# A state-space and expert layer on one core: the last norm's inverse square root joined with two others in the next chunk's group 4, its output added in group 9

## The chip, the cores and the metric

The kernel runs on one core of a Trainium2 chip. The time is device microseconds (us) of one execution. Engines are named as in the profile: PE is the matrix engine (PEld its weight loads), DVE the vector engine, ACT the scalar engine, POOL the GpSimd engine, SP the engine that issues most transfers. All five run their own instruction queue in order and meet at semaphores only.

## What is computed

The input is 8 sequences of 1024 tokens with 256 features in float32. Cut to its core, the reference is

```
x = x + layernorm(mamba(layernorm(x)))      # conv, selective scan, gate, out projection
x = x + layernorm(experts(layernorm(x)))    # 16 experts, 4 of them chosen for each token
layernorm(v) = (v - mean(v)) / sqrt(var(v) + 1e-5)
```

The change touches the outermost norm of the second line, the one behind the experts, and where the sum with x is made.

## The kernel before

The tokens are cut into NC = 16 chunks of 512 tokens, two for each sequence. A chunk lies as 4 blocks (b) of 128 tokens by 256 features, so a statistic of a chunk is a tile of 128x4.

The work is one software pipeline, written out by hand. Every engine runs the same loop over periods p = -2 to 17, and in each over 16 groups g = 0 to 15; G = 16p + g counts the groups. A period carries several chunks at different stages: the scan and its read-out are of chunk p, the input norm (names `e_`) of chunk p + 2, the front part with convolution, dt and gate (names `f_`) of chunk p + 1, the norm and the routing behind the mamba part (names `p_`) of chunk p - 1, the experts run 26 groups behind the scan, and the last norm (names `z_`) was of chunk p - 2. The order inside a group is the order of the `if` lines in each engine's loop; nothing is scheduled automatically. Periods with an odd p are the second half of a sequence and start each scan from the tile carry, periods with an even p save into carry on ACT (L607).

What one group does in the steady state:

- DVE: `expert_gate` (th<-th,Gp, L1007), one scan of 128x512 (L897), `expert_up` (th<-Up,th, L1012), three more scans, then the group's small extras, then `inputs` (L883): hs<-dxr,Bb, 128x2048, which writes the products that the next group scans.
- ACT: four decays dA<-dtr,A (L511) into the two PSUM banks dA0 and dA1, tanh for one expert (L517), and extras. A decay waits until the scan that reads its bank is done.
- POOL: waits until `inputs` of its group is done, then issues the transfer if there is one, weighs one expert (th<-th,cmb, L762) and multiplies the scanned states by C (`read_out`, hs<-hs,Cb, 128x2048, L782). The states read are those of the group before.
- PE: read-out sums, the gate and up products of one expert, the down product of an earlier one, and one projection.

The inverse square root is a bit trick and three Newton steps: `newton` (L813 to L822) is 11 dependent tiny DVE instructions. `variance` (L826) and `shift` (L829) make the input of it and the bias behind it. In group 4, DVE already joins two of them: the two roots of the input norm of chunk p + 2 and the root of chunk p - 1 lie side by side in ep_w, 12 columns, and one `newton` serves all. The `q` root in group 6 stands alone (`p_scale2`).

The last norm of chunk p - 2 before the change, all inside period p: `z_my` in group 11 copies the expert sums from PSUM to my (L674), `z_squares` in group 12 makes the squares (L529, XB<-my,z_s), `z_scale` in group 12 on DVE makes variance, `newton` and shift on z_w with 4 columns, `z_norm` in group 12 on ACT scales my (L685, four instructions), directly ahead of `f_silu_z` (L587, which loads another activation table ahead of it and one behind it), and `add_out` in group 13 on POOL issues the transfer that adds my to the output in DRAM (L772, 512 KB). `z_my` of the next chunk waits until this transfer has landed, since it writes my again.

In group 9, DVE runs `route_groups` and `route_experts` (L944 to L1003) behind the four scans: 31 small instructions on tiles of 128x64 and less in SBUF, which choose the experts; behind them come `y_out` (L904) and `inputs` (L883) of group 10. In ACT's group 8 stand two copies `p_x2T` (L655) with decays and tanh between them.

Of the kernel before, what the change touches and what calls it, by code (L numbers as in the profile page):

```python
# [14 lines left out]
TB = CH // P  # L15
# [60 lines left out]
def sandwich_kernel(nc, x, w_in, w_out, w_gu, w_dn, w_x, w_rt, cols, alog, ebias, consts, sel_dt, out):  # L76
    with ExitStack() as ctx:
# [70 lines left out]
        p_s = sb('p_s', [P, 3, TB])  # L148
        b_s = sb('b_s', [P, 3, TB])
        p_w = sb('p_w', [P, 3, TB])  # L150
        ep_w = sb('ep_w', [P, 3, 3 * TB])
        p_nb = sb('p_nb', [P, TB])
        top8 = sb('top8', [P, TB, 8])
        comb = sb('comb', [P, TB * NE])
# [20 lines left out]
        p_act = Steps(sem('p_act'), ['xn0', 'xn1', 'rev0', 'rev1', 'nm', 'sq', 'ro', 'sum2', 'nm2', 'sq2', 'x2', 'x2T0', 'x2T1', 'sig', 'cmT'])  # L175
        m_g, m_u, m_d, m_th, m_v, m_w, m_a = (sem(k) for k in ('m_g', 'm_u', 'm_d', 'm_th', 'm_v', 'm_w', 'm_a'))
        z_act = Steps(sem('z_act'), ['my', 'nm', 'sq', 'zn'])
        z_dve = Steps(sem('z_dve'), ['w1'] + rsqrt_names('r') + ['nb'])
        ld_w, ld_w2, w_act, w_dve = (sem(k) for k in ('ld_w', 'ld_w2', 'w_act', 'w_dve'))
        ld_xin = sem('ld_xin')  # L180
        ld_x = [sem(f'ld_x{k}') for k in range(2)]
# [316 lines left out]
        def _(act):  # L498
# [45 lines left out]
            def e_norm(c):  # L544
                act.wait_ge(e_dve.sem, e_dve.at(c, 'nbr'))
                for b in range(TB):
                    ins = act.activation(xin[:, b, :], xin[:, b, :], ACT.Identity, scale=ep_w[:, 1, 2 * TB + b:2 * TB + b + 1], bias=e_nb[:, b:b + 1])
                ins.then_inc(e_act.sem, 1)

            def e_xT(p, q):  # L550
# [85 lines left out]
            def p_ro(p):  # L636
                c = p - 1
                act.wait_ge(p_dve.sem, p_dve.at(c, 'nb'))
                for b in range(TB):
                    ins = act.activation(rn[:, b, :], rn[:, b, :], ACT.Identity, scale=ep_w[:, 1, b:b + 1], bias=p_nb[:, b:b + 1])  # L640
                ins.then_inc(p_act.sem, 1)

            def p_x2(p):
# [38 lines left out]
            def z_norm(c):  # L682
                act.wait_ge(z_dve.sem, z_dve.at(c, 'nb'))
                for b in range(TB):
                    ins = act.activation(my[:, b, :], my[:, b, :], ACT.Identity, scale=z_w[:, 1, b:b + 1], bias=z_nb[:, b:b + 1])  # L685
                ins.then_inc(z_act.sem, 1)
            for p, g, G in groups():
                F, R_ = (in_f(p), in_p(p))
                q = expert_at(G)
                if 0 <= p < NC:  # L690
                    decay(G * NBETA + 2)
                    decay(G * NBETA + 3)
                if R_ and g in (3, 4):
# [24 lines left out]
                if R_ and g in (0, 1):  # L718
                    p_xn(p, g)
                if 0 <= p + 2 < NC and g == 2:  # L720
                    e_sums(p + 2)
                if 0 <= p + 2 < NC and g == 3:
                    e_squares(p + 2)
                if R_ and g == 5:
                    p_sums2(p)
                    p_squares2(p)
                if R_ and g == 4:
                    p_ro(p)
                if F and g in (6, 11):
                    f_z(p, {6: 0, 11: 3}[g])  # L730
                if F and g == 6:
                    f_silu(p)
                if R_ and g == 6:
                    p_x2(p)
                if F and g == 7:
                    f_xd(p)
                if in_e(p) and g == 7:
                    e_norm(p + 2)
                if R_ and g == 8:
                    p_x2T(p, 1)  # L740
                if F and g == 9:
                    f_softplus(p)
                if R_ and g == 10:
                    p_cmT(p)
                if g == 11 and 0 <= p - 2 < NC:
                    z_my(p - 2)
                if g == 12 and 0 <= p - 2 < NC:
                    z_norm(p - 2)
                if F and g == 12:
                    f_silu_z(p)  # L750
                if in_e(p) and g == 13:
                    e_xT(p, 0)
                if in_e(p) and g in (14, 15):
                    f_b(p, g - 14)

        @block.gpsimd
        def _(pool):
# [25 lines left out]
            for p, g, G in groups():  # L783
                if 0 <= G < NGRP:
                    pool.wait_ge(s_u, G + 1)
                if in_p(p) and g == 5:
                    add_x1(p - 1)
                if g == 13 and 0 <= p - 2 < NC:
                    add_out(p - 2)
                q = expert_at(G - 2)  # L790
                if q is not None:
# [5 lines left out]
        def _(dve):  # L797
# [33 lines left out]
            def e_var(c):  # L831
                dve.wait_ge(e_act.sem, e_act.at(c, 'sq'))
                if c > 0:
                    dve.wait_ge(e_act.sem, e_act.at(c - 1, 'xr'))
                dve.tensor_scalar(ep_w[:, 0, TB:2 * TB], e_s[:, 1, :], 1.0 / DM, LN_EPS, ALU.mult, ALU.add).then_inc(e_dve.sem, 1)
                dve.tensor_scalar(ep_w[:, 0, 2 * TB:3 * TB], e_s[:, 1, :], (1.0 + RMS_EPS) / DM, LN_EPS * RMS_EPS, ALU.mult, ALU.add).then_inc(e_dve.sem, 1)

            def e_scale(c):
                rs, rr = (ep_w[:, 1, k * TB:(k + 1) * TB] for k in (1, 2))
                dve.tensor_scalar(ln1[:, c, 0, :], rs, 1.0, None, ALU.mult).then_inc(e_dve.sem, 1)  # L840
                dve.tensor_tensor(ln1[:, c, 1, :], e_s[:, 2, :], rs, ALU.mult).then_inc(e_dve.sem, 1)
                dve.tensor_tensor(e_nb[:, :], e_s[:, 2, :], rr, ALU.mult).then_inc(e_dve.sem, 1)
# [178 lines left out]
            for p, g, G in groups():
# [14 lines left out]
                if F and g in (2, 3):  # L1036
                    conv(p, g - 2)
                if g == 4 and (R_ or 0 <= p + 2 < NC):
                    c0, c1 = (0 if R_ else TB, 3 * TB if 0 <= p + 2 < NC else TB)
                    if 0 <= p + 2 < NC:  # L1040
                        e_var(p + 2)
                    if R_:
# [6 lines left out]
                        p_scale(p)  # L1049
                    if 0 <= p + 2 < NC:  # L1050
                        e_scale(p + 2)
                if R_ and g == 6:
                    p_scale2(p)
                if R_ and g == 9:
# [46 lines left out]
```

## Time and profile before

| | us |
|---|---|
| median of 3 runs | 2755.98 |
| lowest and highest of them | 2751.46, 2756.31 |
| the profiled execution, its own time | 2754.25 |
| its span | 2752.5 |
| DVE busy | 2434.5 (88%) |
| PE busy | 2418.8 (88%) |
| ACT busy | 1633.1 (59%) |
| POOL busy | 1511.1 (55%) |

Busy times are of the profiled execution. A period of the steady state takes about 158 us, a group 8 to 13. The rows of a timeline read: start in us from the span's start, duration in us, engine, line, operation, output<-inputs, shapes, count; in brackets the idle time of the engine ahead of it and the engine and line that ended it. Rows of one kind that touch are merged, their start is the first one's.

### The profile page before, as it was taken

Reading aid. Unit: us, or ns where it says so; the run is one execution under the profiler, and the core shown is the slowest. Engines: PE = TensorE matmul, PEld = TensorE weight load, DVE = VectorE, ACT = ScalarE, POOL = GpSimd, SP = SyncE. Lnnn points to the kernel's source line nnn. Section 1 sums busy time; section 2 is a strip of 40 time slices with the busy share of each in tenths; the row PEclk is TensorE's granted clock in tenths of the full one; section 3 lists DMA queues with packets and bytes.
Section 4 is the critical chain, followed back from the end, with each engine's and each line's share of the span. In section 5 each row is a group of like instructions: output and inputs, shape, how many; then the busy total and the mean of one; then the engine's idle time right before and its main releaser. Section 6 shows DMA issues by size and latency. Waiting matters only on the chain.

```text
span 2752.5 us, 27115 instructions
## 1 busy us (share of the span) xinstructions
PE 2418.8 (88%) x8416; PEld 1183.5 (43%) x8416; DVE 2434.5 (88%) x3233; ACT 1633.1 (59%) x3312; POOL 1511.1 (55%) x548
## 2 busy tenths in 40 slices
PE   4556799998989999998999999898999989888987
PEld 1112254453545444444544445453544545443554
DVE  1699999999999999999999999999999999999532
ACT  3565656666665667566566667666566666644321
POOL 0255565655556565655656565565656555565422
PEclk9777899999999999999999999999999999999999
DMA  1623253534344343524435353443535343442232
GB/s 35 231 86 124 94 177 93 180 118 153 114 134 155 118 158 118 183 87 156 140 115 177 101 176 109 144 137 103 186 93 179 118 155 105 137 157 80 68 87 56
DMA packets 175563, 353.43 MB, mean 128 GB/s; under 512 B 16283, under 2 KB 82108, under 8 KB 166972
## 3 DMA queue, kind: packets, MB, share of 16 engines
q1 hardware_dynamic: 164668, 334.93, 36.3%
q0 software_dynamic: 10752, 16.78, 3.7%
q8 instruction: 67, 1.10, 0.2%
q14 instruction: 76, 0.62, 0.1%
HBM read 291.35 MB, written 51.90 MB: 125 GB/s over the span
## 4 chain that ended last, share of the span: by engine, by line
DVE 57%; issue 19%; ACT 15%; PE 7%; POOL 1%; DMA 1%; DVEq 0%; SPq 0%; POOLq 0%; ACTq 0%
DVE hs L897 26%; DVE hs L883 12%; DVE th L1007 5%; DVE th L1012 4%; ACT DX L529 2%; DVE XC L856 2%; PE Gp L424 2%; ACT dA L511 1%; ACT L511 1%; PE Up L432 1%; PE FP L351 1%; PE FP L361 1%; ACT XC L582 1%; ACT SZ L587 1%; ACT XB L529 1%
## 5 line engine op out<-in xcount | busy, mean ns | idle before, releaser
L782 POOL TENSOR_TENSOR hs<-hs,Cb 128x2048 f32<-128x2048 f32 x256 | 1170.6, 4572 | 199.8 <-DVE hs L883 199.8
L511 ACT ACTIVATE dA<-dtr,A 128x512 f32<-128x512 f32 x1024 | 701.8, 690 | 827.9 <-DVE hs L897 826.9
L762 POOL TENSOR_TENSOR th<-th,cmb 128x512 f32<-128x512 f32 x256 | 338.1, 1325 | 803.4 <-DVE hs L883 711.8
L897 DVE TENSOR_TENSOR_SCAN hs<-dA,carry,hs 128x512 f32<-128x512 f32 x512 | 627.7, 1265 | 19.8 <-ACT dA L511 19.4
L424 PE MATMUL Gp<-x2T,Wgu 128*128 128x512 f32 x1024 | 532.6, 645 | 115.2 <-DVE th L1007 115.1
L897 DVE TENSOR_TENSOR_SCAN hs<-dA,hs 128x512 f32<-128x512 f32 x512 | 596.1, 1203 | 31.6 <-ACT dA L511 31.1
L883 DVE TENSOR_TENSOR hs<-dxr,Bb 128x2048 f32<-128x2048 f32 x256 | 601.9, 2351 | 12.5 <-DMA dxr<-dx_d 12.5
L432 PE MATMUL Up<-x2T,Wgu 128*128 128x512 f32 x1024 | 492.7, 604 | 0.0
L442 PE MATMUL MY<-Wdn,th 128*128 128x256 f32 x2048 | 486.4, 380 | 0.2 <-POOL th L762 0.2
L442 PEld LDWEIGHTS MY<-Wdn,th 128*128 128x128 f32 x2048 | 383.5, 190 | 137.4 <-issue 94.7
L424 PEld LDWEIGHTS Gp<-x2T,Wgu 128*128 128x128 f32 x1024 | 182.2, 196 | 449.5 <-issue 253.6
L351 PE MATMUL FP<-xT,Win 128*128 128x512 f32 x512 | 270.2, 653 | 74.1 <-ACT XB L601 40.3
L432 PEld LDWEIGHTS Up<-x2T,Wgu 128*128 128x128 f32 x1024 | 196.4, 196 | 265.0 <-issue 227.6
L454 PE MATMUL Y<-hs,Cst 128*32 128x512 f32 x2048 | 283.2, 626 | 27.4 <-POOL hs L782 27.4
L1007 DVE SCALAR_TENSOR_TENSOR th<-th,Gp 128x512 f32<-128x512 f32 x256 | 173.6, 678 | 73.6 <-ACT th L517 73.6
L517 ACT ACTIVATE th<-Gp 128x512 f32<-128x512 f32 x256 | 148.3, 579 | 88.7 <-PE Gp L424 88.7
L351 PEld LDWEIGHTS FP<-xT,Win 128*128 128x128 f32 x512 | 98.0, 203 | 222.2 <-issue 99.5
L1012 DVE TENSOR_TENSOR th<-Up,th 128x512 f32<-128x512 f32 x256 | 170.2, 665 | 10.5 <-PE Up L432 10.0
L387 PE MATMUL FP<-Wout,SZ 128*128 128x256 f32 x512 | 123.9, 386 | 6.1 <-ACT DX L622 6.1
L361 PE MATMUL FP<-XB,Kdiag 128*128 128x512 f32 x256 | 120.4, 614 | 6.1 <-ACT XB L560 6.1
L387 PEld LDWEIGHTS FP<-Wout,SZ 128*128 128x128 f32 x512 | 99.0, 194 | 35.0 <-issue 15.7
L454 PEld LDWEIGHTS Y<-hs,Cst 128*32 128x32 f32 x2048 | 40.8, 109 | 155.2 <-issue 113.3
(131 smaller groups left out, 1820.5 us busy)
## 6 DMA issues: line engine op xcount, KB each, us to landing
dtr<-dt_d SPq DMA_DIRECT2D x64, 1024.0 KB, 5.7
dxr<-dx_d SPq DMA_DIRECT2D x128, 512.0 KB, 7.5
cmb<-cm_d SPq DMA_DIRECT2D x256, 256.0 KB, 3.7
Wdn<-in_w_dn SPq DMA_DIRECT2D x256, 128.0 KB, 3.6
dt_d<-XB SPq DMA_DIRECT2D x16, 1024.0 KB, 4.3
dx_d<-DX SPq DMA_DIRECT2D x16, 1024.0 KB, 5.9
Bb<-bc_d SPq DMA_DIRECT2D x64, 256.0 KB, 3.0
Cb<-bc_d SPq DMA_DIRECT2D x64, 256.0 KB, 4.0
```

What stands on the lines that cost most here:

```text
L351: mm = pe.matmul(FP[:, :], Win[:, q, c0:c0 + P], xT[:, q, :], start=q == 0, stop=q == KM - 1)
L424: mm = pe.matmul(Gp[:, :], Wgu[:, k, e, 0:DE], x2T[:, c % 2, k, :], start=k == 0, stop=k == KM - 1)
L432: mm = pe.matmul(Up[:, :], Wgu[:, k, e, DE:2 * DE], x2T[:, c % 2, k, :], start=k == 0, stop=k == KM - 1)
L442: mm = pe.matmul(MY[b // 2][:, (b % 2) * DM:(b % 2 + 1) * DM], th[:, q % NTH, b * P:(b + 1) * P], Wdn[:, q % NWD, :], start=e == 0 and b % ...
L454: mm = pe.matmul(Y[beta * CB:(beta + 1) * CB, :], sel_y, hs[:, G % NH, beta, :], start=False, stop=s == NSIG - 1, tile_position=(0, beta * ...
L511: act.activation(dA[h % 2][:, :], dtr[:, M % 2, beta, :], ACT.Exp, scale=A[:, k:k + 1]).then_inc(s_dA, 1)
L762: pool.tensor_tensor(th[:, q % NTH, :], th[:, q % NTH, :], cmb[:, q % 2, :], ALU.mult).then_inc(m_a, 1)
L782: pool.tensor_tensor(hs[:, G % NH, :, :], hs[:, G % NH, :, :], Cb[:, s, :].unsqueeze(1).broadcast_to([P, NBETA, CH]), ALU.mult).then_inc(s ...
L883: dve.tensor_tensor(hs[:, G % NH, :, :], dxr[:, M % 2, :, :], Bb[:, s, :].unsqueeze(1).broadcast_to([P, NBETA, CH]), ALU.mult).then_inc(s_ ...
L897: dve.tensor_tensor_scan(hv, dA[h % 2][:, :], hv, first, ALU.mult, ALU.add).then_inc(s_h, 1)
L1007: dve.scalar_tensor_tensor(out=th[:, q % NTH, :], in0=th[:, q % NTH, :], scalar=1.0, in1=Gp[:, :], op0=ALU.add, op1=ALU.mult).then_inc(m_v, 1)
L1012: dve.tensor_tensor(th[:, q % NTH, :], Up[:, :], th[:, q % NTH, :], ALU.mult).then_inc(m_w, 1)
```

## The change

The tile ep_w gets 16 columns instead of 12. The two roots of chunk p + 2 move to columns 0 to 7, the root of chunk p - 1 to columns 8 to 11, and columns 12 to 15 take the root of the last norm of chunk p - 3. For chunks 0 to 13, `z_scale` in group 12 is gone from DVE: variance is made in group 4 of the next period, the joined `newton` serves it too, and the shift is made behind the others. `z_norm` moves from group 12 to group 8 of the next period on ACT, and `add_out` from group 13 to group 9 of the next period on POOL, ahead of the weighing and the read-out of that group. The last two chunks stay as they were.

```diff
-        ep_w = sb('ep_w', [P, 3, 3 * TB])
+        ep_w = sb('ep_w', [P, 3, 4 * TB])
...
             def z_norm(c):
                 act.wait_ge(z_dve.sem, z_dve.at(c, 'nb'))
                 for b in range(TB):
-                    ins = act.activation(my[:, b, :], my[:, b, :], ACT.Identity, scale=z_w[:, 1, b:b + 1], bias=z_nb[:, b:b + 1])
+                    rs = z_w[:, 1, b:b + 1] if c >= NC - 2 else ep_w[:, 1, 3 * TB + b:3 * TB + b + 1]
+                    ins = act.activation(my[:, b, :], my[:, b, :], ACT.Identity, scale=rs, bias=z_nb[:, b:b + 1])
...
-                if g == 12 and 0 <= p - 2 < NC:
+                if g == 8 and 0 <= p - 3 < NC - 2:
+                    z_norm(p - 3)
+                if g == 12 and NC - 2 <= p - 2 < NC:
                     z_norm(p - 2)
...
-                if g == 13 and 0 <= p - 2 < NC:
+                if g == 9 and 0 <= p - 3 < NC - 2:
+                    add_out(p - 3)
+                if g == 13 and NC - 2 <= p - 2 < NC:
                     add_out(p - 2)
...
                 if g == 4 and (R_ or 0 <= p + 2 < NC):
-                    c0, c1 = (0 if R_ else TB, 3 * TB if 0 <= p + 2 < NC else TB)
+                    Z = 0 <= p - 3 < NC - 2
+                    c0, c1 = (0 if 0 <= p + 2 < NC else 2 * TB, (4 if Z else 3 if R_ else 2) * TB)
+                    if Z:
+                        z_var(p - 3, ep_w[:, :, 3 * TB:])
+                        dve.wait_ge(z_dve.sem, z_dve.at(p - 3, 'w1'))
...
+                    if Z:
+                        shift(z_dve, z_nb, z_s, ep_w[:, :, 3 * TB:])
...
-                if g == 12 and 0 <= p - 2 < NC:
+                if g == 12 and NC - 2 <= p - 2 < NC:
                     z_scale(p - 2)
```

The order of the instructions at the places that matter follows; line numbers of the changed kernel are 1 to 6 higher than before.

POOL in period 3, groups 8 to 12 and the start of 13, before. L762 is the weighing, L782 the read-out, L772 the transfer of the last norm:

```order
L762 TENSOR_TENSOR th<-th,cmb 128x512
L782 TENSOR_TENSOR hs<-hs,Cb 128x2048
L762 TENSOR_TENSOR th<-th,cmb 128x512
L782 TENSOR_TENSOR hs<-hs,Cb 128x2048
L762 TENSOR_TENSOR th<-th,cmb 128x512
L782 TENSOR_TENSOR hs<-hs,Cb 128x2048
L762 TENSOR_TENSOR th<-th,cmb 128x512
L782 TENSOR_TENSOR hs<-hs,Cb 128x2048
L762 TENSOR_TENSOR th<-th,cmb 128x512
L782 TENSOR_TENSOR hs<-hs,Cb 128x2048
L772 DMA out<-my 128x4x256
L762 TENSOR_TENSOR th<-th,cmb 128x512
```

and the same queue now, groups 8 to 10 of period 3 (L766, L786 and L776 are the same three):

```order
L766 TENSOR_TENSOR th<-th,cmb 128x512
L786 TENSOR_TENSOR hs<-hs,Cb 128x2048
L776 DMA out<-my 128x4x256
L766 TENSOR_TENSOR th<-th,cmb 128x512
L786 TENSOR_TENSOR hs<-hs,Cb 128x2048
L766 TENSOR_TENSOR th<-th,cmb 128x512
L786 TENSOR_TENSOR hs<-hs,Cb 128x2048
```

The transfer stood ahead of the weighing of group 13; it now stands ahead of that of group 9, one period later.

ACT now, from the first x2T copy of group 8 to the sigmoid's exponential of group 9, in period 3 (before, the same rows without L687):

```order
L656 ACTIVATE x2T<-FP 128x512
L512 ACTIVATE dA<-dtr,A 128x512 x2
L518 ACTIVATE th<-Gp 128x512
L656 ACTIVATE x2T<-FP 128x512
L687 ACTIVATE my<-my,z_nb,ep_w 128x256 x4
L512 ACTIVATE dA<-dtr,A 128x512 x2
L661 ACTIVATE DX<-FP 128x64
```

The four instructions of `z_norm` stand behind the last extra of group 8, ahead of group 9's decays. In group 12 they are gone from between tanh (or the save into carry) and the table load of `f_silu_z`.

DVE now, group 4 of period 3, from the last scan to the start of the joined root:

```order
L903 SCALAR_TENSOR_TENSOR hs<-dA,carry,hs 128x512 [waits s_dA] x3
L832 TENSOR_SCALAR ep_w<-z_s 128x4 [waits z_act]
L841 TENSOR_SCALAR ep_w<-e_s 128x4 [waits e_act,z_dve]
L842 TENSOR_SCALAR ep_w<-e_s 128x4
L832 TENSOR_SCALAR ep_w<-p_s 128x4 [waits p_act]
L819 TENSOR_SCALAR ep_w<-ep_w 128x16 [waits e_dve,p_dve]
```

The first L832 is new, ahead of the other three inputs; the joined root has 16 columns instead of 12, and one L835 (z_nb<-z_s,ep_w) is new behind the other results, directly ahead of `inputs`.

## Rows read from the trace of the kernel before

**Rows 1.** The page: the chain of waits that ended last, shares by engine.

```profile
DVE 57%; issue 19%; ACT 15%; PE 7%; POOL 1%; DMA 1%; DVEq 0%; SPq 0%; POOLq 0%; ACTq 0%
```

**Rows 2.** Groups by line, then waits (total us, times, longest): z_norm.

```profile
L685 ACT ACTIVATE my<-my,z_nb,z_w 128x256 f32<-128x256 f32 x64 | 33.2, 589 | 16.8 <-DVE z_nb L829 16.8
...
ACT my L685 <- DVE z_nb L829: 16.8, 16, 2.6
```

**Rows 3.** Timeline, groups 12 and 13 of an even period.

```profile
1439.59 4.53 POOL L782 TENSOR_TENSOR hs<-hs,Cb 128x2048 f32<-128x2048 f32 x1
...
1444.72 0.17 DVE L826 TENSOR_SCALAR z_w<-z_s 128x4 f32<-128x4 f32 x1 [0.77 <-ACT XB L529]
...
1446.29 0.20 ACT L607 ACTIVATE carry<-hs 128x4 f32<-128x4 f32 x1
...
1447.18 2.28 DVE L883 TENSOR_TENSOR hs<-dxr,Bb 128x2048 f32<-128x2048 f32 x1
1447.30 2.07 ACT L685 ACTIVATE my<-my,z_nb,z_w 128x256 f32<-128x256 f32 x4 [0.81 <-DVE z_nb L829]
...
1449.39 1.28 ACT L587 ACT_TABLE_LOAD   x1
...
1450.02 1.33 POOL L772 DMA_DIRECT2D out<-my  x1 [5.90 <-DVE hs L883]
...
1452.09 5.03 POOL L782 TENSOR_TENSOR hs<-hs,Cb 128x2048 f32<-128x2048 f32 x1
...
1454.63 2.34 DVE L897 TENSOR_TENSOR_SCAN hs<-dA,hs 128x512 f32<-128x512 f32 x2 [1.73 <-ACT dA L511]
```

**Rows 4.** Timeline, groups 8 and 9 of an odd period.

```profile
1562.11 0.59 ACT L655 ACTIVATE x2T<-FP 128x512 f32<-128x512 f32 x1
...
1564.46 4.53 POOL L782 TENSOR_TENSOR hs<-hs,Cb 128x2048 f32<-128x2048 f32 x1
...
1564.98 0.69 ACT L511 ACTIVATE dA<-dtr,A 128x512 f32<-128x512 f32 x1 [2.28 <-DVE hs L897]
...
1568.98 0.17 DVE L944 TENSOR_SCALAR DX<-DX 128x64 f32<-128x64 f32 x1
...
1569.77 0.22 DVE L948 TENSOR_TENSOR DX<-DX,Ebias 128x64 f32<-128x64 f32 x1
```

**Rows 5.** Timeline, groups 8 and 9 of an even period.

```profile
1403.71 0.58 ACT L655 ACTIVATE x2T<-FP 128x512 f32<-128x512 f32 x1
...
1406.10 4.53 POOL L782 TENSOR_TENSOR hs<-hs,Cb 128x2048 f32<-128x2048 f32 x1
...
1410.40 0.29 DVE L944 TENSOR_SCALAR DX<-DX 128x64 f32<-128x64 f32 x1
```

**Rows 6.** Timeline, group 5 of an even period: a late read-out and inputs.

```profile
421.20 4.80 POOL L782 TENSOR_TENSOR hs<-hs,Cb 128x2048 f32<-128x2048 f32 x1
...
423.76 4.40 DVE L883 TENSOR_TENSOR hs<-dxr,Bb 128x2048 f32<-128x2048 f32 x1
```

**Rows 7.** Timeline, inputs in group 13 of period 15.

```profile
2555.42 3.40 DVE L883 TENSOR_TENSOR hs<-dxr,Bb 128x2048 f32<-128x2048 f32 x1
```

**Rows 8.** Groups by line: a step of the joined root; waits: DVE in group 4.

```profile
L820 DVE TENSOR_TENSOR ep_w<-ep_w 128x12 f32<-128x12 f32 (+2 forms) x57 | 9.6, 169 | 1.9
...
DVE ep_w L826 <- ACT DX L529: 28.8, 16, 6.9
```

**Rows 9.** Timeline, period 16 (no scans): group 8 on ACT, routing on DVE.

```profile
2634.86 0.60 ACT L655 ACTIVATE x2T<-FP 128x512 f32<-128x512 f32 x1 [1.56 <-PE FP L397]
...
2638.54 0.20 DVE L944 TENSOR_SCALAR DX<-DX 128x64 f32<-128x64 f32 x1 [3.42 <-ACT DX L660]
```

**Rows 10.** Timeline, groups 12 and 13 of period 16: no read-out behind the transfer.

```profile
2663.77 2.07 ACT L685 ACTIVATE my<-my,z_nb,z_w 128x256 f32<-128x256 f32 x4 [2.13 <-DVE z_nb L829]
...
2667.06 3.00 POOL L762 TENSOR_TENSOR th<-th,cmb 128x512 f32<-128x512 f32 x2
```

**Rows 11.** The transfer of the last norm (line L772): from issue to landing.

```profile
DMA to landing us min/median/max: 5.8/12.9/14.1
```

More of the change, by code:

```diff
@@ L177, in sandwich_kernel @@
         z_act = Steps(sem('z_act'), ['my', 'nm', 'sq', 'zn'])
-        z_dve = Steps(sem('z_dve'), ['w1'] + rsqrt_names('r') + ['nb'])
+        z_dve = Steps(sem('z_dve'), ['w1', 'nb'])
+        y_dve = Steps(sem('y_dve'), rsqrt_names('r'))
         ld_w, ld_w2, w_act, w_dve = (sem(k) for k in ('ld_w', 'ld_w2', 'w_act', 'w_dve'))
@@ L546, in e_norm @@
                 for b in range(TB):
-                    ins = act.activation(xin[:, b, :], xin[:, b, :], ACT.Identity, scale=ep_w[:, 1, 2 * TB + b:2 * TB + b + 1], bias=e_nb[:, b:b + 1])
+                    ins = act.activation(xin[:, b, :], xin[:, b, :], ACT.Identity, scale=ep_w[:, 1, TB + b:TB + b + 1], bias=e_nb[:, b:b + 1])
                 ins.then_inc(e_act.sem, 1)
@@ L639, in p_ro @@
                 for b in range(TB):
-                    ins = act.activation(rn[:, b, :], rn[:, b, :], ACT.Identity, scale=ep_w[:, 1, b:b + 1], bias=p_nb[:, b:b + 1])
+                    ins = act.activation(rn[:, b, :], rn[:, b, :], ACT.Identity, scale=ep_w[:, 1, 2 * TB + b:2 * TB + b + 1], bias=p_nb[:, b:b + 1])
                 ins.then_inc(p_act.sem, 1)
@@ L834, in e_var @@
                     dve.wait_ge(e_act.sem, e_act.at(c - 1, 'xr'))
-                dve.tensor_scalar(ep_w[:, 0, TB:2 * TB], e_s[:, 1, :], 1.0 / DM, LN_EPS, ALU.mult, ALU.add).then_inc(e_dve.sem, 1)
-                dve.tensor_scalar(ep_w[:, 0, 2 * TB:3 * TB], e_s[:, 1, :], (1.0 + RMS_EPS) / DM, LN_EPS * RMS_EPS, ALU.mult, ALU.add).then_inc(e_dve.sem, 1)
+                dve.tensor_scalar(ep_w[:, 0, 0:TB], e_s[:, 1, :], 1.0 / DM, LN_EPS, ALU.mult, ALU.add).then_inc(e_dve.sem, 1)
+                dve.tensor_scalar(ep_w[:, 0, TB:2 * TB], e_s[:, 1, :], (1.0 + RMS_EPS) / DM, LN_EPS * RMS_EPS, ALU.mult, ALU.add).then_inc(e_dve.sem, 1)
             def e_scale(c):
-                rs, rr = (ep_w[:, 1, k * TB:(k + 1) * TB] for k in (1, 2))
+                rs, rr = (ep_w[:, 1, k * TB:(k + 1) * TB] for k in (0, 1))
                 dve.tensor_scalar(ln1[:, c, 0, :], rs, 1.0, None, ALU.mult).then_inc(e_dve.sem, 1)
@@ L907, in p_var @@
                 dve.wait_ge(p_act.sem, p_act.at(p - 1, 'sq'))
-                variance(p_dve, p_s, ep_w)
+                variance(p_dve, p_s, ep_w[:, :, 2 * TB:3 * TB])
             def p_scale(p):
-                shift(p_dve, p_nb, p_s, ep_w)
+                shift(p_dve, p_nb, p_s, ep_w[:, :, 2 * TB:3 * TB])
             def p_scale2(p):
@@ L1012, in expert_up, with z_var @@
                 dve.tensor_tensor(th[:, q % NTH, :], Up[:, :], th[:, q % NTH, :], ALU.mult).then_inc(m_w, 1)
+            def z_var(c, w):
+                dve.wait_ge(z_act.sem, z_act.at(c, 'sq'))
+                variance(z_dve, z_s, w)
             def z_scale(c):
-                dve.wait_ge(z_act.sem, z_act.at(c, 'sq'))
-                variance(z_dve, z_s, z_w)
+                z_var(c, z_w)
                 dve.wait_ge(z_dve.sem, z_dve.at(c, 'w1'))
-                newton(z_dve, c, 'r', z_w)
+                newton(y_dve, c - (NC - 2), 'r', z_w)
                 shift(z_dve, z_nb, z_s, z_w)
```

## The prediction, made before the changed kernel ran

> **What bounds the kernel now.** I read the page's chain of waits first: 57% of it is DVE, 19% issue time between instructions, 15% ACT [rows 1]. So DVE sets the pace, and ACT takes over in a few groups. Then I looked in the timeline for the groups in which the last norm stands, first group 12, where it is, then 4, 8 and 9, where it goes. What a step is worth there depends on which engine is late behind it.
>
> Group 12 is one of the few where ACT takes over [rows 3]. DVE's scans end at 1443.95; it idles 0.77 us until ACT's squares are done, makes the root and the shift from 1444.72 on and then, at 1447.18, `inputs`. ACT is free at 1446.49 (behind the save into carry), waits 0.81 us for the shift, scales my for 2.07 us and only then, at 1449.39, loads the table for the gate's silu. Everything behind that load is late: the third scan of group 13 waits 1.73 us for its decay and starts at 1454.63. Both engines are held by the same step.
>
> Group 9 looks harmless and is not. In an odd period routing starts on DVE at 1568.98, and POOL's read-out ends at 1568.99 [rows 4]. In an even one the read-out ends at 1410.63, and the first routing instruction, started at 1410.40, takes 0.29 instead of 0.17 us [rows 5]: it ends just behind the read-out. That this is a block and no coincidence shows in group 5 [rows 6]: a read-out runs to 426.00, and `inputs`, started at 423.76, takes 4.40 instead of the 2.28 us of rows 3, so it ends 2.16 us behind POOL's end. The price is the overlap less 0.12 us (2.24 - 0.12 = 2.12 = 4.40 - 2.28). The scans, which read the decay from PSUM, run under the read-out without it: all three behind 1564.98 do. So POOL's long instructions run under scans, and DVE's work on SBUF alone starts when they end, by a hair.
>
> **The change, part by part.**
>
> *Group 12 loses the root and the scaling (14 times, periods 2 to 15).* DVE would start `inputs` at about 1443.95. The read-out runs to 1444.12 [rows 3], so it takes 2.28 + 0.05 us and ends near 1446.3. The expert gate behind it waits for tanh, which stands right ahead of the save on ACT and ends when that starts, by 1446.4; today it starts with the end of `inputs` at 1449.4. On ACT the table load starts where the save ends, 1446.5 instead of 1449.39. Both engines come 2.9 us sooner, and the wait of 1.73 us for the decay stays. An odd period has no save but the same tie. From the group's sum: of the idle time of 16.8 us, 2.13 and 2.6 us belong to the two chunks that stay [rows 2, 10], so 12.1 us go; a scaling is 33.2 / 16 = 2.07 us [rows 2]: 12.1 + 14 x 2.07 = 41.1 us. **-41.1.**
>
> *Period 15, group 13.* The transfer's issue is what pushes that read-out into `inputs`, which takes 3.40 us instead of 2.28 [rows 7]. Without the issue POOL ends sooner. **-1.1.**
>
> *Group 4 gets one variance, four columns and one shift.* The variance stands ahead of the wait for ACT's squares, and DVE idles there 28.8 us in 16 periods [rows 8], so it is hidden; without that cover it would cost the 0.2 us of a step and its wait. The shift costs at most the 0.17 us of such a step [rows 8]; with the columns and its overlap with the instruction ahead of it I take 0.12 us, in the 7 odd periods. In an even one the read-out of group 5 ends late by ACT's clock and holds `inputs` anyway [rows 6], which takes it up. Between 0 and 14 x 0.2 = 2.8; **+0.8.**
>
> *Group 8 gets the scaling on ACT.* ACT's x2T copy ends at 1562.70, and the next decay waits 2.28 us for a scan, until 1564.98 [rows 4]. Four scalings take 2.07 us and end at about 1564.67. Hidden, with 0.3 us to spare. In the even period the copy ends at 1404.29 [rows 5], the scaling at about 1406.26. With that cover gone it would cost the 2.07 us.
>
> *Group 9 gets the transfer on POOL (13 times with a read-out, periods 3 to 15).* POOL's queue is in order: the issue now waits for the scaling, until 1564.67, and the weighing and the read-out stand behind it. In rows 3 the issue starts 0.56 us behind the end of `inputs`, and the read-out ends (1457.12) 7.10 us behind the issue's start. For the lag I take 0.45 us, so POOL starts at 1565.12 and its read-out ends at 1572.22, instead of 1568.99 [rows 4]. Routing is ready at 1568.98 and held: 1572.22 - 1568.98 - 0.12 = 3.12 us. In the even period POOL starts at 1406.71 and ends at 1413.81: 1413.81 - 1410.40 - 0.12 = 3.29, less the 0.12 already paid, 3.17 us [rows 5]. DVE alone sets the pace there, so group 10's `inputs` comes as much later. 7 x 3.12 + 6 x 3.17: **+40.9.**
>
> These small instructions overlap a read-out by 0.25 us at most today, so the rows bound the price rather than give it: nothing, if the small ones are not really held, up to the whole 3.3 us. The middle: if instructions with one SBUF input pass and the first with two (at 1569.77, 0.79 us later) is held, it is 2.3 us. I take the whole, because L944 with its single input does end behind POOL in all seven even periods.
>
> The Trainium skill (SBUF — State Buffer, section "SBUF: two separate sides") speaks against this move: the vector engine and GpSimd share one port pair, locked for a whole instruction, and the vector engine needs it with two SBUF inputs or in a two-port mode. The trace agrees as far as rows 6 go. Without such a lock the sum would be a gain of 41 us, with it nothing. The page's other warning, that a transfer issued from GpSimd starves while the vector engine holds the port, would lengthen the landing only.
>
> *Period 16* has no read-out, but the scaling ends near 2637.5 (behind the copy of 2634.86), the issue follows at 2637.9, and the two weighings behind it hold POOL for 3.00 us [rows 10] from about 2638.7, when routing has just started at 2638.54 [rows 9]. Nothing hides routing there. Between nothing and 3.0; I take the upper end, as in group 9. **+3.0.**
>
> *The landing* takes 5.8 to 14.1 us [rows 11]; from group 9 to the next write of my in group 11 a normal period leaves over 30 us, period 16 some 19. Hidden.
>
> Sum: -41.1 - 1.1 + 0.8 + 40.9 + 3.0 = +2.5 us on the profiled execution's 2754.25, so **2756.8 us**. That execution lies 1.7 us under the median of the runs shown, so the forecast is 0.8 us above that median. 0.2%, 5.5 us, is about what a measurement of this kernel can tell from no change.
>
> **The rivals.**
>
> *No block: the gain stays (9%).* The 0.29 us of L944 was chance, or POOL yields between short instructions. Then +40.9 and +3.0 fall away: -41.4, 2712.9 us. Against it speak rows 5 and 6; for it, that no small instruction of today overlaps a read-out for long.
>
> *Half a block (13%).* Only instructions with two SBUF inputs are held: 13 x 0.79 = 10.3 us less, 2746.5 us. Against it speaks the single input of L944.
>
> *A block in group 12 as well (14%), the slower side.* Today DVE idles 0.77 us and runs its root between the last scan and `inputs`; that is what lets POOL's read-out end first. Without it `inputs` starts within 0.2 us of the read-out's end, and whatever makes POOL late there is paid in full. From 0.2 us of lateness in each of 14 periods on, the kernel is slower by over 0.2% (2.5 + 2.8). With the 1.1 us of rows 7 in each it would be 2756.8 + 15.4 = 2772 us. Against it: no transfer stands in group 12, before or after.
>
> *The gain in group 12 is smaller (6%)*, because something that the trace hides is next behind the silu: at 2 instead of 2.9 us, 2770 us.
>
> **How the numbers follow.** The forecast has 58%: its own spread is 13 times some 0.3 us of lag, 4 us, so 46 points of it lie within 0.2%, 11 above and 1 below. Faster: 9 + 13 + 1 = 23%. Same: 46, and 3 of the milder blocks in group 12, 49%. Slower: 11 + 11 + 6 = 28%. The range goes from 2742 (half a block, less a spread) to 2772 (the slower rival); left out are the 9% without a block and some tails. The likeliest case alone is 2751 to 2762.
>
> **What would show it.** Right: the table load of group 12 follows tanh or the save directly, and DVE no longer idles ahead of `inputs` there; in group 9 the first routing instruction (L944 before) takes some 3.3 us instead of 0.2 and ends with the read-out, whose end lies 7.1 us behind the issue of the transfer; a period stays as long as it was. A routing instruction of 0.2 us while a read-out runs would make the block wrong, and a period 3 us shorter the sum. A third scan of group 13 that starts without a wait, or `inputs` of over 2.5 us in group 12, would speak for the last two rivals.

## The result, and the profile after

| | before | after |
|---|---|---|
| median, us (5 runs each) | 2754.32 | 2770.64 |
| lowest and highest | 2751.46, 2756.31 | 2764.78, 2774.54 |
| the profiled execution, its own time | 2754.25 | 2774.54 |
| its span | 2752.5 | 2772.8 |

The ratio is 1.0058 with a 95% interval of 1.0046 to 1.007: slower by 0.58%, 16.3 us by the medians. It lies within the range of the forecast (2742 to 2772), but not where its likeliest case put it, at 2756.8 and within 0.2%. The two profiled executions differ by 20.3 us, and all terms below are of these two; that of the changed kernel is the slowest of its five.

The page of the changed kernel, the chain by engine. Against [rows 1], PE's share has doubled, from 7 to 15%, and DVE's has fallen from 57 to 50%. Nothing in the prediction says why.

```profile
DVE 50%; issue 17%; PE 15%; ACT 15%; DMA 1%; POOL 1%; SPq 0%; DVEq 0%; POOLq 0%; ACTq 0%
```

**Group 12**, timeline of ACT and DVE in groups 12 and 13 of an even period (start, duration, engine, line; idle time and its releaser in brackets), which answers to [rows 3]:

```profile
1454.34 2.40 DVE L889 TENSOR_TENSOR hs<-dxr,Bb 128x2048 f32<-128x2048 f32 x1
...
1456.76 0.19 ACT L608 ACTIVATE carry<-hs 128x4 f32<-128x4 f32 x1
1456.97 1.28 ACT L588 ACT_TABLE_LOAD   x1
...
1462.21 2.34 DVE L903 TENSOR_TENSOR_SCAN hs<-dA,hs 128x512 f32<-128x512 f32 x2 [1.79 <-ACT dA L512]
```

`inputs` follows the scans at once and takes 2.40 us (2.27 in odd periods, 2.28 before), the table load follows the save at once, and the wait for the decay is still there (1.79 us, before 1.73). From one `inputs` to the next, group 12 is 3.2 to 3.3 us shorter than before in each of the 14 periods and group 13 longer by 0.2 to 0.4.

**Group 9**, timeline of ACT, POOL and DVE, first an even period, then an odd one, which answer to [rows 5] and [rows 4]:

```profile
1411.23 2.07 ACT L687 ACTIVATE my<-my,z_nb,ep_w 128x256 f32<-128x256 f32 x4
...
1413.95 1.34 POOL L776 DMA_DIRECT2D out<-my  x1 [4.27 <-issue]
...
1414.80 1.79 POOL L766 TENSOR_TENSOR th<-th,cmb 128x512 f32<-128x512 f32 x1
...
1416.03 5.03 POOL L786 TENSOR_TENSOR hs<-hs,Cb 128x2048 f32<-128x2048 f32 x1
...
1417.42 3.69 DVE L950 TENSOR_SCALAR DX<-DX 128x64 f32<-128x64 f32 x1
```

```profile
1570.29 2.06 ACT L687 ACTIVATE my<-my,z_nb,ep_w 128x256 f32<-128x256 f32 x4
...
1573.01 1.32 POOL L776 DMA_DIRECT2D out<-my  x1 [4.40 <-issue]
...
1575.07 5.02 POOL L786 TENSOR_TENSOR hs<-hs,Cb 128x2048 f32<-128x2048 f32 x1
...
1576.69 3.46 DVE L950 TENSOR_SCALAR DX<-DX 128x64 f32<-128x64 f32 x1
```

The first routing instruction takes 3.69 and 3.46 us instead of 0.29 and 0.17. Its end, 1421.11 and 1580.15, lies 0.05 and 0.06 us behind that of the read-out. Over the whole execution it is one row of the groups by line:

```profile
L950 DVE TENSOR_SCALAR DX<-DX 128x64 f32<-128x64 f32 x16 | 50.4, 3147 | 3.4 <-ACT DX L661 3.4
```

**Where the 20.3 us come from**, by the starts of all 256 `inputs` in both traces:

| stretch | predicted | measured |
|---|---|---|
| groups 12 and 13, 14 periods | -41.1 | -41.0 |
| period 15, the later `inputs` | -1.1 | -1.1 |
| group 4 | +0.8 | +1.5 |
| group 9, 13 periods | +40.9 | +43.8 |
| behind the last `inputs` (period 16) | +3.0 | +5.5 |
| groups 1, 2, 6 and 7 | 0 | +10.4 |
| ahead of and in group 0 of period 0 | 0 | +1.3 |

The last row is no effect of the change: in the other kernels below it lies between -3.1 and +2.5. The stretch behind the last `inputs` scatters too, by up to 1.0 us: it is 0.9 and 1.0 us longer than before in kernels 2 and 11 below, which change nothing in period 16. The row above it is the surprise. Groups 2 and 6 are longer in 8 periods (4, 6, 7, 8, 10, 11, 12 and 14) and not in the others. The waits of the changed kernel (total us, times, longest) say for whom:

```profile
ACT XB L561 <- PE FP L352: 75.5, 45, 3.9
ACT XC L572 <- PE FP L362: 59.7, 28, 5.6
```

Before, these two were 32.9 and 43.7 us. Here FP is the PSUM tile of PE's projections, and ACT waits for it before it copies out. So PE is late against the others, in some periods. The timeline shows it in group 2 of period 8:

```profile
1342.26 0.69 ACT L572 ACTIVATE XC<-FP,Cols 128x512 f32<-128x512 f32 x1 [3.22 <-PE FP L362]
```

```profile
1344.54 2.34 DVE L903 TENSOR_TENSOR_SCAN hs<-dA,hs 128x512 f32<-128x512 f32 x2 [0.61 <-ACT dA L512]
```

### The profile page after: what moved, and what is told of

Its sections match the earlier page's. It is cut to its first block, busy times and chain, and to the rows that moved or that the text cites. A ratio compares the mean times of both kernels' runs of the same rounds, so it can differ in the third digit from the quotient of the medians.

```text
span 2772.8 us, 26964 instructions
## 1 busy us (share of the span) xinstructions
PE 2423.5 (87%) x8416; PEld 1182.7 (43%) x8416; DVE 2463.0 (89%) x3079; ACT 1632.4 (59%) x3312; POOL 1511.4 (55%) x548
## 4 chain that ended last, share of the span: by engine, by line
DVE 50%; issue 17%; PE 15%; ACT 15%; DMA 1%; POOL 1%; SPq 0%; DVEq 0%; POOLq 0%; ACTq 0%
DVE hs L903 23%; DVE hs L889 10%; DVE th L1013 4%; DVE th L1018 4%; PE Gp L425 3%; PE Up L433 3%; PE FP L352 3%; ACT dA L512 2%; PE FP L362 2%; PE MY L443 2%; DVE DX L950 2%; ACT DX L530 2%; DVE XC L862 2%; PE Y L455 2%; ACT L512 1%
## 5 line engine op out<-in xcount | busy, mean ns | idle before, releaser
L786 POOL TENSOR_TENSOR hs<-hs,Cb 128x2048 f32<-128x2048 f32 x256 | 1170.6, 4573 | 200.9 <-DVE hs L889 200.9
L766 POOL TENSOR_TENSOR th<-th,cmb 128x512 f32<-128x512 f32 x256 | 337.9, 1326 | 828.8 <-DVE hs L889 740.8
L889 DVE TENSOR_TENSOR hs<-dxr,Bb 128x2048 f32<-128x2048 f32 x256 | 608.1, 2376 | 12.1 <-DMA dxr<-dx_d 12.1
L425 PE MATMUL Gp<-x2T,Wgu 128*128 128x512 f32 x1024 | 519.6, 631 | 71.7 <-DVE th L1013 71.6
L433 PE MATMUL Up<-x2T,Wgu 128*128 128x512 f32 x1024 | 485.3, 596 | 0.0
L455 PE MATMUL Y<-hs,Cst 128*32 128x512 f32 x2048 | 297.1, 654 | 30.0 <-POOL hs L786 29.9
L452 PE MATMUL Y<-XC,Ddiag 128*128 128x512 f32 x128 | 83.4, 740 | 55.9 <-DVE SZ L910 55.6
```

Of the source, the lines that this page charges most:

```text
L425: mm = pe.matmul(Gp[:, :], Wgu[:, k, e, 0:DE], x2T[:, c % 2, k, :], start=k == 0, stop=k == KM - 1)
L433: mm = pe.matmul(Up[:, :], Wgu[:, k, e, DE:2 * DE], x2T[:, c % 2, k, :], start=k == 0, stop=k == KM - 1)
L455: mm = pe.matmul(Y[beta * CB:(beta + 1) * CB, :], sel_y, hs[:, G % NH, beta, :], start=False, stop=s == NSIG - 1, tile_position=(0, beta * ...
L766: pool.tensor_tensor(th[:, q % NTH, :], th[:, q % NTH, :], cmb[:, q % 2, :], ALU.mult).then_inc(m_a, 1)
L786: pool.tensor_tensor(hs[:, G % NH, :, :], hs[:, G % NH, :, :], Cb[:, s, :].unsqueeze(1).broadcast_to([P, NBETA, CH]), ALU.mult).then_inc(s ...
L889: dve.tensor_tensor(hs[:, G % NH, :, :], dxr[:, M % 2, :, :], Bb[:, s, :].unsqueeze(1).broadcast_to([P, NBETA, CH]), ALU.mult).then_inc(s_ ...
```

## The experiments

Two questions were open. Is the price of group 9 the block of the prediction, and nothing else? And where do the 10.4 us of the other groups come from? For the second I had first two theories, "slack" (shortening group 12 takes away the time in which PE catches up) and "delay" (the block of group 9 shifts PE against DVE). Each kernel was timed beside the kernel before, 4 to 11 executions of each, and ratios are to that, with 95% intervals.

**1. The transfer issued behind the read-out.**

```
 # POOL, group 9
-if g == 9: add_out(p - 3)
 weigh(q)
 read_out(G - 1)
+if g == 9: add_out(p - 3)
```

> As the change, but in group 9 POOL issues the output's transfer behind its weighing and read-out, not ahead of them, so nothing on POOL waits for the scaling. Theory 'block': the 3.4 us of group 9 are the read-out's lateness alone, so all 13 of them go (-43.8), and the three of the tail (-3). Where groups 2 and 6 became longer (about +10 us in the change) there are two causes to choose from. Theory 'slack': shortening group 12 takes away the time in which TensorE catches up, so the +10 stay: 2770.6 - 43.8 - 3 = about 2724 us. Theory 'delay': the block of group 9 shifts TensorE against VectorE, so the +10 go with it: about 2714 us. If the block isn't the price, the time stays above 2750.

Measured: 2724.34 us, ratio 0.9896 (0.9881 to 0.9912). Group 9 is as long as before (all 13 together -0.2 us). One even period, timeline:

```profile
1392.22 4.54 POOL L786 TENSOR_TENSOR hs<-hs,Cb 128x2048 f32<-128x2048 f32 x1
...
1396.51 0.31 DVE L950 TENSOR_SCALAR DX<-DX 128x64 f32<-128x64 f32 x1
...
1396.69 1.34 POOL L776 DMA_DIRECT2D out<-my  x1
...
1396.86 0.55 DVE L952 RECIPROCAL DX<-DX 128x64 f32<-128x64 f32 x1
```

Routing runs on under the issue itself, unslowed (the reciprocal takes 0.55 us in every period before too); it is only the late read-out that holds it. Groups 1, 2, 6 and 7 keep most of their growth (7.2 us, in 7 periods). "Slack" fits, "delay" does not.

**2. A wait in group 9 of the kernel before.**

```
+if g == 9 and 3 <= p < NC:
+    pool.wait_ge(s_dA, G * NBETA + 3)
```

> The kernel before, with one wait more: in group 9 of periods 3 to 15 POOL waits for the group's third decay before it weighs, which makes its read-out about 2.45 us late (decay ends at 1565.67, weighing started at 1563.23 before). No norm and no transfer is moved. Theory 'block': routing is held that long, 13 x 2.45 = +32 us, 2786 us, and the first routing instruction takes some 2.6 us. Theory 'slack': groups 2 and 6 stay as they were. Theory 'delay': they grow as in the change, some 7 us more, 2793 us. If instructions with one SBUF input aren't held, the first takes 0.2 us and the whole is about +20.

Measured: 2786.98 us, ratio 1.0117 (1.0104 to 1.0131). Group 9 is 2.4 or 2.5 us longer in each of the 13 periods, 31.9 us together, and the other groups are as they were, to 0.2 us in all. With neither the norm nor the transfer moved, a late read-out alone makes the price, as expected to 0.2 us:

```profile
1416.38 1.26 POOL L762 TENSOR_TENSOR th<-th,cmb 128x512 f32<-128x512 f32 x1 [4.74 <-ACT dA L511]
...
1417.60 4.51 POOL L782 TENSOR_TENSOR hs<-hs,Cb 128x2048 f32<-128x2048 f32 x1
...
1419.39 2.78 DVE L946 TENSOR_SCALAR DX<-DX 128x64 f32<-128x64 f32 x1
```

It ends at 1422.17, the read-out at 1422.11. And "delay" is out from its other side: a block without the shorter group 12 lets nothing grow.

**3. The transfer at the head of group 10.**

```
-if g == 9 and 0 <= p - 3 < NC - 2:
+if g == 10 and 0 <= p - 3 < NC - 2:
     add_out(p - 3)
```

> As the change, with the issue of the output's transfer ahead of the weighing in group 10 instead of 9. The scaling is long done then, so POOL waits for nothing, only the issue itself (some 1.2 us) stands ahead of the read-out. Group 9's 3.4 us go (-43.8 - 3). Theory 'block': the read-out of group 10 ends 1.2 us late and holds the next inputs by about 1.2, as the transfer did in group 13 of period 15 (3.40 instead of 2.28): 13 x 1.2 = +15.6, about 2740 us. Rival: the read-out of group 10 has room, and the time is that of the kernel with the issue behind the read-out.

Measured: 2744.08 us, ratio 0.9959 (0.9947 to 0.9972). Group 10 is 1.5 to 1.8 us longer in 12 of the 13 periods (19.4 in all) and as long as before in period 15. The block holds there too; an issue ahead of a read-out costs 0.3 to 0.6 us more than the 1.2 expected. The growth of groups 2 and 6 came in 4 periods only.

**4. Chunk 13 left where it was.** As 1, with `NC - 3` for `NC - 2` in each condition.

> As the kernel with the issue behind the read-out, but chunk 13 too keeps its norm in group 12 of period 15 and its transfer in group 13, so that period 16 has nothing new. Costs 2.9 + 1.1 = 4.0 us in period 15. If the +5.5 us behind the last inputs come from the wait of POOL alone, the other kernel has lost them already and this one is 4 us slower; if they come from the scaling on ACT, this one is about 1.5 us faster.

Measured: 2727.16 us, ratio 0.9903 (0.9889 to 0.9916). Neither of the two: period 15 costs the 4.1 us, but the stretch behind the last `inputs` is 3.7 us shorter than in kernel 1, which had kept 3.6 of the 5.5 us. The reason is in the timeline of kernel 1, period 16:

```profile
2604.17 1.34 POOL L776 DMA_DIRECT2D out<-my  x1 [6.93 <-ACT my L687]
2605.01 1.80 POOL L766 TENSOR_TENSOR th<-th,cmb 128x512 f32<-128x512 f32 x1
```

```profile
2604.92 1.95 DVE L950 TENSOR_SCALAR DX<-DX 128x64 f32<-128x64 f32 x1 [3.42 <-ACT DX L661]
```

```profile
2614.24 3.62 PE L425 MATMUL Gp<-x2T,Wgu 128*128 128x512 f32 x4 [4.36 <-DVE th L1013]
```

Without scans the groups follow each other fast: the issue waits for the scaling even behind its own group, and the weighing of the next one stands behind it and holds routing by 1.8 us. PE idles 4.36 us meanwhile, where it idled 2.62 before the change, and its four matmuls then take 3.62 us instead of 1.96: the other 1.7.

**5. The transfer into x1 between weighing and read-out; in period 16 the scaling one group earlier.** As 1, and

```
-if in_p(p) and g == 5: add_x1(p - 1)
 weigh(q)
+if in_p(p) and g == 5: add_x1(p - 1)
 read_out(G - 1)
```

> The kernel with the issue behind the read-out, with two places changed. First, in period 16 the scaling stands in ACT's group 7 instead of 8: there the issue waited for it ahead of the next weighing, and the stretch behind the last inputs is 3.6 us longer than before; expected -3.5. Second, in group 5 of each period POOL issues the transfer into x1 between its weighing and its read-out, not ahead of both: it waits there for the normed read-out anyway, and the weighing of 1.2 us can run meanwhile. Theory 'block': the inputs of 4.42 us (even) and 3.65 us (odd) become 1.2 to 1.3 us shorter, 14 or 15 times: -18. Together 2724 - 3.5 - 18 = about 2703 us. Rival: the weighing delays the transfer, and ACT's sums over x1 then come later and take the gain back: about 2720.

Measured: 2721.29 us, ratio 0.9878 (0.9863 to 0.9893). The second edit did what was expected: the stretch behind the last `inputs` is 187.3 us, before the change 187.8. The first gave nothing; the rival was right. In period 7, where PE's clock (below) is at its full value in both kernels, the `inputs` that ends group 5 does get shorter, from 2.71 to 2.48 us. But the transfer now starts later and ACT's sums over x1 wait for it; the third scan behind them waits 1.31 instead of 0.44 us, and group 6 takes 12.2 instead of 11.5 us:

```profile
1207.03 0.42 ACT L522 ACTIVATE DX<-x 128x256 f32<-128x256 f32 x1 [0.53 <-DMA x<-DX]
```

```profile
1211.70 2.46 DVE L903 TENSOR_TENSOR_SCAN hs<-dA,carry,hs 128x512 f32<-128x512 f32 x2 [1.31 <-ACT dA L512]
```

**What tells the periods apart.** Having kernels with growth in some periods, I compared a period with and one without in kernel 1, engine by engine, from group 9 on. The first difference is PE's clock. Windows over groups 12, 13 and 14 (busy time and instructions of PE, PEld, DVE, ACT, POOL; granted clock; DMA), first without growth behind it, then with:

```profile
1267.30:1275.40 8.10, 8.10 (x31) 4.18 (x30) 8.10 (x8) 6.02 (x19) 5.75 (x3) 1.00 0.32 89
1275.40:1286.00 10.60, 8.04 (x34) 4.06 (x32) 8.86 (x9) 9.31 (x14) 5.81 (x3) 1.00 0.64 222
1286.00:1294.20 8.20, 6.88 (x24) 2.77 (x25) 8.20 (x9) 3.83 (x7) 5.76 (x2) 1.00 0.49 160
```

```profile
1422.00:1430.00 8.00, 8.00 (x30) 3.99 (x30) 8.00 (x8) 6.01 (x20) 5.77 (x3) 1.00 0.33 107
1430.00:1440.70 10.70, 8.21 (x35) 4.26 (x33) 8.76 (x9) 9.54 (x15) 6.02 (x3) 1.00 0.65 225
1440.70:1448.60 7.90, 6.51 (x20) 2.50 (x21) 7.90 (x9) 3.84 (x8) 5.53 (x2) 0.78 0.52 159
```

In group 14 the granted clock is 0.78 instead of 1.00, that is, part of the stretch at 1.2 instead of 2.4 GHz. The slow matmuls are the first difference in time as well: in kernel 1 the even periods 6 and 8 agree to 0.01 us up to PE's first matmul of group 14, 1.38 us behind the start of `inputs`, and then the expert gate's product of the next group comes at 4.02 us without a drop (6) and at 5.61 us with one (8). Now the same stretch in the kernel before and in the changed one, one period each, groups 13 and 14:

```profile
1289.60:1300.00 10.40, 7.46 (x20) 3.94 (x20) 8.79 (x9) 8.99 (x11) 7.10 (x3) 0.84 0.65 186
1300.00:1308.10 8.10, 6.91 (x25) 2.77 (x25) 8.10 (x8) 3.80 (x7) 5.72 (x2) 1.00 0.96 283
```

```profile
1294.90:1305.60 10.70, 8.06 (x34) 4.09 (x32) 8.96 (x10) 9.41 (x14) 5.82 (x3) 1.00 0.66 229
1305.60:1313.70 8.10, 6.86 (x21) 2.49 (x22) 8.10 (x9) 3.75 (x7) 5.76 (x2) 0.79 0.47 152
```

Before, the clock falls too, in every period from 2 to 13, but one group earlier. PE's rows of the kernel before and of the changed one show what it did ahead of that:

```profile
1292.54 3.42 PE L424 MATMUL Gp<-x2T,Wgu 128*128 128x512 f32 x4 [4.04 <-DVE th L1007]
```

```profile
1306.84 0.66 PE L342 MATMUL FP<-Cst,xin 128*128 128x128 f32 x4 [2.80 <-ACT xT L553]
1307.34 1.28 PE L452 MATMUL Y<-XC,Ddiag 128*128 128x512 f32 x2
```

The held-up group 12 made PE idle 4.04 us waiting for the gate; the slow matmuls behind it (3.42 instead of 1.98 us) lay under the wait of DVE for the decay. With group 12 shorter this idle time is gone, and PE idles one group later, for ACT's copy of xT, in a place from which it is on the critical path: in the changed kernel 1.4 to 1.6 us of lateness there cost DVE 0.5 to 0.7 us in group 2 and 0.4 to 0.9 in group 6 (in period 3, where the clock of group 14 is 0.58, 2.9 us of lateness cost 1.4 and 0.9). Over periods 2 to 13 of kernels 1, 3, 4 and 5, of kernels 7 and 8 below, and of the change itself, the clock of group 14 is under 0.8 in 48 of 84 cases. Group 2 of the next period is longer by 0.4 to 1.4 us behind each of these 48, and by nothing behind the other 36. So "slack" had to be amended to "clock": a drop that used to be hidden now stands where nothing covers it. The Trainium skill (TensorE: Matmul & The Clock Gate, Part 1) says that PE's array falls to half rate by idling and asks for short gaps. The rows agree that the drops stand behind idle time, 4.04 and 2.80 us here; that a drop is free in one group and costs in the next is this kernel's own.

The trace of the kernel before had an example of this already. Its period 1 carries no last norm, so nothing holds up group 12, and PE's gap stands in group 14:

```profile
350.51 0.82 PE L341 MATMUL FP<-Cst,xin 128*128 128x128 f32 x4 [1.98 <-ACT xT L552]
```

The granted clock of that group is 0.79, and group 2 of period 2 takes 10.85 us, where that of period 4 takes 10.15. All eight kernels here without an extra matmul in the gap show this drop in period 1.

**6. PE's gap filled with work.** As 1; the first matmul into Y of group 14 moved into group 13:

```
 # PE, group 13
 down(q)
+start_y(G - 1)        # Y = Ddiag x XC, was first in group 14
 e_turn(p, 1)
```

> The kernel with the issue behind the read-out, with the first matmul into Y (1.0 us) taken from the start of group 14 to TensorE's idle time in group 13, ahead of the second transposition of the inputs. There TensorE idles 2.93 us, and in 7 of 12 periods its granted clock falls to 0.79 in the next group; just behind these 7, and no other, groups 2 and 6 are longer (together 7.2 us). Theory 'clock': with the idle time cut to about 1.8 us the clock stays at 1.00 and the growth goes: about 2717 us. Theory 'slack alone': the clock is as before, and 1.0 us more of slack takes back part of the growth, to about 2720. Rival: the growth has nothing to do with either, 2724.

Measured: 2715.49 us, ratio 0.9856 (0.9842 to 0.9869). The gap is 1.69 us:

```profile
1437.30 1.13 PE L451 MATMUL Y<-XC,Ddiag 128*128 128x512 f32 x2 [1.69 <-DVE SZ L916]
1438.53 0.66 PE L342 MATMUL FP<-Cst,xin 128*128 128x128 f32 x4
```

The growth is all but gone (groups 1, 2, 6 and 7 together -1.1 us against before). The clock falls in 2 periods of 12 instead of 7, and behind these two group 2 isn't longer either, while group 6 is in one of them, by 0.5 us: the expert gate's product of group 14 now starts 0.8 to 0.9 us sooner. Both halves of the expectation were partly right.

**7. The same matmul twice**, once for nothing in the gap and once in its place:

```
+start_y(G - 1, stop=True)   # group 13
 e_turn(p, 1)
 ...
 start_y(G)                  # group 14, as before
```

> The kernel with the issue behind the read-out, with that matmul into Y made twice: once more, for nothing, in TensorE's idle time in group 13, and again in its old place, where it overwrites the first. No work is saved or moved on any path; TensorE is only busy 1.0 us longer in the gap. Theory 'clock': the granted clock of group 14 stays at 1.00 and groups 2 and 6 lose their growth, about 2717 us. Theory 'slack alone': 2724 us or a little more, clock as before.

Measured: 2717.69 us, ratio 0.9869 (0.9856 to 0.9883). The 2717 us of "clock" by the number. In the trace the drop is rarer, 4 periods of 12, not gone, and groups 2 and 6 grow behind these 4 alone (3.0 us with groups 1 and 7). Since kernel 3 had 4 too without the matmul, this alone wouldn't prove that the work prevents the drop. Together the kernels say more: 44 drops in 72 periods without a matmul in the gap (the change and kernels 1, 3, 4, 5 and 8), 8 in 48 with it (6, 7, 9 and 10).

**8. The scaling in group 7, the issue still ahead in group 9.** The change, and

```
-if g == 8 and 0 <= p - 3 < NC - 2:
+if g == 7 and 0 <= p - 3 < NC - 2:
     z_norm(p - 3)
```

> The change, with the scaling in ACT's group 7 instead of 8, and the issue still ahead of the weighing in group 9. It separates the wait of the issue from the issue itself. Theory 'block': POOL no longer waits, only the issue (1.2 to 1.3 us) stands ahead of the read-out, so routing is held 1.2 us instead of 3.4: 13 x 2.1 = 27 us less than the change, about 2742 us, and the tail's 3 us go as well. ACT's scaling of 2.07 us in group 7 may stick out where a norm of the next inputs stands too: up to 14 x 1 us more. If the issue alone were the price, it stays near 2770.

Measured: 2751.88 us, ratio 0.9992 (0.9983 to 1.0001), 10 more than expected. Group 9 costs 20.4 us, 1.4 to 1.7 a period: that is the issue without the wait, and the wait was the other 23. But group 8 is now longer by 9.9 us in all (0.6 to 0.9 in ten periods, 2.6 in period 4): ACT's scaling pushes a decay, and the third scan waits for it.

```profile
1399.06 2.06 ACT L687 ACTIVATE my<-my,z_nb,ep_w 128x256 f32<-128x256 f32 x4
...
1401.73 2.34 DVE L903 TENSOR_TENSOR_SCAN hs<-dA,hs 128x512 f32<-128x512 f32 x2 [0.81 <-ACT dA L512]
```

So group 8 is the right place for the scaling, as the prediction had costed it: in the change the groups 8 together are longer by less than 0.1 us. The clock of group 14 fell in 9 periods here, and groups 1, 2, 6 and 7 grew by 12.1 us.

**9. The parts that paid, together**: kernel 6, with the scaling of period 16 one group earlier.

> The parts that paid, together: the roots joined, the output's transfer issued behind the read-out, the first matmul into Y in TensorE's gap of group 13, and in period 16 the scaling in ACT's group 7. The last took 4.2 us from the stretch behind the last inputs in the run that had it (187.2 instead of 191.5). Expected 2715.5 - 4 = about 2711.5 us. Rival: that stretch was shorter by chance, 2715.5.

Measured: 2709.99 us, ratio 0.9843 (0.983 to 0.9857): 1.6% under the kernel before.

**10. The change with the matmul of kernel 6**, for the term that the sum had not held.

> The change itself, its block in group 9 and all, with the first matmul into Y in TensorE's gap of group 13. Theory 'clock and slack': the part that the prediction's sum did not hold, the 10 us of groups 2 and 6, goes almost whole: 2770.6 - 9 = about 2762 us. If those 10 us came with the block of group 9, they stay: 2770.

Measured: 2761.25 us, ratio 1.0029 (1.0018 to 1.0039). Group 9 costs 43.6 us as in the change, the clock of group 14 is 1.00 in all twelve periods, and groups 1, 2, 6 and 7 have lost their growth (-1.6 us against before). By the ratios, 1.0058 and 1.0029, the matmul is worth 8 us to the change, by the medians 9. Nor does this rest on one execution of each: the mean granted clock is 0.951 to 0.955 in the five of the change and 0.956 to 0.960 in the eight of this kernel. So most of the 10 us of the change are this.

**11. The kernel before with that matmul alone.**

> The kernel before with only that matmul moved. There the clock falls in group 13, right behind the idle time of group 12, and groups 2 and 6 never wait for TensorE. Theory: the move is worth nothing by itself, 2754 us within 0.2%. Rival: it shortens a path of its own, and the gain of about 8 us seen with the change has nothing to do with group 12: 2746 us.

Measured: 2752.94 us, ratio 0.9997 (0.9988 to 1.0006). Worth nothing that a time can show; its clock falls in group 13 as ever. In the trace the matmul takes 1.4 us from period 2, whose predecessor is the one with a short group 12 and now keeps its clock at 1.00, and nothing from the others. It pays only where group 12 is short.

## Why the prediction was right and wrong

*Group 12, -41.1.* Right to the tenth (-41.0), from two engines held by one step, and so was period 15 (-1.1). Both rivals that lived on it, a block in group 12 as well and a smaller gain, are out: `inputs` takes at most 2.41 us there.

*Group 9, +40.9.* Right in mechanism and in full. "No block" and "half a block" are out: L950 has one SBUF input and is held to the end, and kernels 1 and 2 show the price both taken away and put in by itself. The size was 2.9 us low, by the lag: I took 0.45 us from the scaling's end to the issue, and it is 0.62 to 0.78 in the 13 periods, 0.68 in the mean (1413.30 to 1413.95, 1572.35 to 1573.01), with a read-out that ends 7.1 us behind the issue's start, as forecast.

*Group 8, hidden.* Right, under 0.1 us. *Group 4, +0.8.* 1.5: the shift costs 0.1 us in even periods too. *The landing.* Hidden, and short besides.

*Period 16, +3.0.* Too small, 5.5. The block is as forecast (L950 takes 3.17 us), but the step ended there. PE waits for what routing holds up, and pays for its idle time:

```profile
2663.98 3.75 PE L425 MATMUL Gp<-x2T,Wgu 128*128 128x512 f32 x4 [5.59 <-DVE th L1013]
```

These matmuls took 1.96 us before, behind a gap of 2.62. The 3.0 us of routing and 1.8 of slow matmuls are 4.8 of the 5.5 us; the rest is within the scatter of that stretch.

*"A period stays as long as it was".* This is the step that failed, and it made the case of 49%, no change, into a slowdown. For group 9, "DVE alone sets the pace there" was right; the sum went wrong where it took group 12's gain as complete once DVE and ACT had been followed. I followed each moved piece to DVE, ACT and POOL, and treated PE, with 7% of the chain [rows 1], as out of the game: its term is missing, without a reason given. The sum had 2.5 us; 10.4 came from the clock drop that the shorter group 12 moves from group 13 to group 14, 2.9 from the lag, 2.5 from period 16 and 0.7 from group 4. With the 1.3 us at the start, that is 20.3. The forecast's own spread, 4 us for 13 lags, would have held the error of the lag and no more. Of the slower side the prediction had 28%, for other reasons than the true one. That 2770.64 lies in the range at all is luck: the likeliest case ended at 2762, and the range went to 2772 for a block in group 12 that isn't there.

## What to carry to other kernels

A step may move to a place where the engine that executes it is idle and still be paid in full: what counts is what stands behind its DMA's issue on POOL's queue, and whether DVE works in SBUF while that runs. Put an issue that may wait behind the long POOL instruction, not ahead of it; here this one line turned +0.6% into -1.0%. And when a stall is taken out of one group, look where the engines that used to idle in it will idle next: a clock drop hidden under the old stall can come out from under it, and a piece of work that is due anyway, moved into the new gap, takes it back.

## What the runs showed of the hardware

- DVE's small instruction with a single SBUF input is held by POOL's read-out like the large one with two: 3.46 and 3.69 us instead of 0.17, ending 0.05 to 0.07 us behind it. Scans that read their decay from PSUM run under the same read-out: the one ahead of routing in kernel 1 takes its usual 1.19 us under one. The issue of a transfer on POOL (1.34 us) holds nothing on DVE.
- An issue of 1.33 us on POOL ahead of a read-out that DVE waits for makes the group 1.4 to 1.8 us longer (kernels 3 and 8): the weighing right behind it takes 1.79 instead of 1.27 us, and the read-out 5.03 instead of 4.53.
- The same transfer of 512 KB lands in 5.6, 6.0 and 6.4 us (least, median, most) with 14 of its 16 issues in group 9, where it took 5.8, 12.9 and 14.1 with all of them in group 13 [rows 11]. Why is open.
- PE's clock falls behind a gap of 3.9 to 4.0 us in each of 12 periods, behind one of 2.8 to 2.9 us in 4 to 9 of them by kernel, and behind 1.7 us in none, 2, 2 and 4. Yet in period 1 it falls behind 2.0 us in all eight kernels with that gap, so the length of the one gap doesn't decide. What decides it from period to period stays open.
